# The transposes of a per-pixel convolution on one Trainium2 core: in pieces of four, on a new timetable

## Chip, core and metric

The kernel runs on one core of one Trainium2 chip. The engines of the core have an instruction stream each and meet only at semaphores: TensorE (PE in the rows, with its weight loads as PEld), VectorE (DVE), ScalarE (ACT), GpSimd (POOL) and the DMA queue of SyncE (SP). The metric is the device time of one execution in microseconds, the median over runs.

## What is computed

Eight images of 128 channels and 128 x 128 pixels pass through two layers. The first (a windowed attention and a pointwise network) isn't touched. The second, cut to its core:

```python
enh  = conv_depthwise_3x3(conv1x1(x))                   # 128 channels
h    = conv_grouped_3x3(x); h1, h2 = split(h)           # 8 and 8 channels
att  = conv1x1(h1 * h2) * attgamma + conv1x1'(x)        # 16 coefficients a pixel
# a kernel of its own at each pixel: 64 groups of 2 channels, 9 taps
attk = einsum('bpn,nm->bpm', att, selfw)                # p = pixel
y    = einsum('bpgij,bpgj->bpgi', attk, patches(enh)) + einsum('bpn,nc->bpc', att, selfb)
out  = y * ga1 + enh + x
```

The sum over taps and over the two channels of a group is what the change touches.

## The kernel before

The convolution stage works in 64 bands of 16 rows, eight to an image. A band has 4 chunks (index `j`) of 4 rows, 512 pixels, one PSUM bank. With 9 taps that makes 36 kernels, numbered `q = 9 * j + tap`. For each `q`:

- TensorE makes the pixel kernels in two matmuls of 512 columns (`basis_kernels`, L1022), into one of only two double banks `ps_k`, one half for each of the two channels of a group;
- VectorE multiplies them with the shifted `enh` (`product`, L1247), 128 x 1024 values. For 10 of the 36 (`VECTOR_MERGES`) the product stays in `ps_k` and a second VectorE instruction adds it to the next product (`merge`, L1253). The others are stored in one of 13 places of `products`. Six pairs (`POOL_MERGES`) are added up by GpSimd (L946);
- the 20 stored results that are left, the **terms**, are added up by TensorE: it transposes each row of a term into the PSUM bank `ps_t` of the chunk, accumulating (`add_term`, L1039). A term has two halves of four rows. The half `s = 0` is turned by `ident`, the half `s = 1` by `ident_swap`, which swaps the two channels. After the last term of a chunk come four transposes of `x` itself (`x_own`, L1047). This is the residual. ScalarE copies the finished bank to `summedT` (L1137), TensorE turns it back and adds the bias (`back`, L1054 and L1056), ScalarE copies it to `out_sb` (L1142), and SyncE stores it.

VectorE's 46 instructions of a band (36 products, 10 merges) are the clock of the stage. Their places 0 to 45 are the **slots**. The kernel `q` may be made as soon as its double bank is free, so it stands in the slot of the instruction that frees it (`KERNEL_SLOT`). K0 to K35 are the 36 pairs of matmuls below.

All engines work on several bands at once, in a software pipeline of four parts: band `l` is loaded, `m` gets its coefficients and `enh`, `n` is convolved, `o` is finished. In what order an engine issues its work is fixed by tables of slots:

- TensorE goes through the slots 0 to 45 and issues in each: the kernels of the slot, the terms whose `TERM_SLOT` it is (both halves, eight transposes in a row), the `back` of `BACK_SLOTS`, two matmul groups of the grouped convolution for each entry of `CONV_SLOTS` (L1004; the profile shows four records for an entry, since each of these matmuls makes two passes), the coefficients (L1011) in slot 28, and a pointwise chunk (L981) in each of `PW_SLOTS`. A number of 46 or more means the next step.
- ScalarE sorts its work by place. `TAP_PLACES` has the 18 tap products of the depthwise convolution (L1157 and L1162), and the copies of sums and outputs follow one slot after their matmuls.
- GpSimd adds 16 taps a band (L940), at places 0 to 15, and its six merges stand between them by `POOL_MERGE_PLACES`.
- Everything waits by counting semaphores. The wait stands in front of the instruction, and each engine runs in order, so that whatever stands behind it waits too.

## Time and profile before

| | us |
|---|---|
| median of 3 runs | 5569.37 (5568.04 to 5569.73) |
| profiled execution: device time | 5569.1 |
| its span, first to last instruction | 5567.0 |
| TensorE busy | 5405.1 (97%) |
| VectorE busy | 5175.4 (93%) |
| GpSimd busy | 4224.4 (76%) |
| ScalarE busy | 3301.8 (59%) |

The first 1900 us are the first layer. The convolution stage fills the rest, 64 bands one after the other. The mean granted clock of TensorE over the span is 0.996 of full speed. A VectorE instruction's duration in the rows is longer than the distance to the next start, so distances from start to start tell more than durations and idle times do.

### The profile page before, as it was taken

The numbers are of one execution on the slowest core, as the hardware profiler recorded it, in microseconds if no ns is written. First come the engines' busy times: TensorE is split into PE (matmuls) and PEld (weight loads), VectorE is DVE, ScalarE is ACT, GpSimd is POOL, SyncE is SP. The second block draws the span as 40 slices with busy tenths as digits, with TensorE's granted clock in tenths as the row PEclk, the third lists the DMA queues.
The fourth block names the chain that finished last, engine by engine and source line by source line (L and its number), as shares of the span: only waits on it lengthen the run. The fifth ranks groups of instructions, "written<-read, shape, count | busy, mean of one in ns | idle before, by whom it ended". The sixth has DMA issues, their size and how long they took to land.

```text
span 5567.0 us, 112695 instructions
## 1 busy us (share of the span) xinstructions
PE 5405.1 (97%) x37904; PEld 3895.4 (70%) x37904; DVE 5175.4 (93%) x5424; ACT 3301.8 (59%) x4094; POOL 4224.4 (76%) x1958
## 2 busy tenths in 40 slices
...
GB/s 94 71 75 75 75 75 75 70 74 75 75 75 64 78 74 79 73 78 70 81 68 75 75 73 79 73 79 68 80 70 72 81 73 78 69 82 67 72 80 46
DMA packets 175615, 413.21 MB, mean 74 GB/s; under 512 B 37200, under 2 KB 58768, under 8 KB 175504
## 3 DMA queue, kind: packets, MB, share of 16 engines
...
q14 instruction: 18, 0.15, 0.0%
...
## 4 chain that ended last, share of the span: by engine, by line
PE 45%; DVE 17%; issue 4%; DVEq 0%; DMA 0%; ACT 0%
PE ps_k L1022 19%; PE ps_t L1039 12%; DVE products L1247 10%; PE ps_m L1004 8%; DVE products L1253 4%; PE ps_p L981 3%; PE ps_t L1047 2%; PE ps_t L1056 1%; DVE ps_k L1247 1%; PE ps_t L1054 1%; DVE h_prod L1267 1%; DVEq L120 0%; DVE products L1216 0%; DMA edge_rows<-products 0%; DVE basis L329 0%
## 5 line engine op out<-in xcount | busy, mean ns | idle before, releaser
L940 POOL TENSOR_TENSOR enh<-enh,tap 128x1024 f32<-128x1024 f32 x1024 | 2258.6, 2206 | 431.3 <-ACT tap L1162 393.1
L1247 DVE TENSOR_TENSOR products<-ps_k,enh 128x1024 f32<-128x1024 f32 x1664 | 2002.9, 1219 | 71.9 <-PE ps_k L1022 36.9
L1022 PE MATMUL ps_k<-att,basis 128*128 128x512 f32 x4608 | 1710.8, 457 | 105.3 <-DVE products L1247 42.6
L1022 PEld LDWEIGHTS ps_k<-att,basis 128*128 128x128 f32 x4608 | 713.1, 189 | 873.9 <-DVE products L1247 553.4
L473 POOL TENSOR_TENSOR hidden_lo<-hidden,hidden_hi 128x1024 fp32r<-128x1024 f32 x256 | 692.8, 2726 | 717.7 <-DVE hidden_hi L678 717.7
L1162 ACT ACTIVATE tap<-e,dw 128x1024 f32<-128x1024 f32 x1024 | 1137.0, 1142 | 7.9 <-POOL enh L940 7.9
L946 POOL TENSOR_TENSOR products<-products 128x1024 f32<-128x1024 f32 x384 | 915.2, 2383 | 118.6 <-DVE products L1247 118.6
L1247 DVE TENSOR_TENSOR ps_k<-ps_k,enh 128x1024 f32<-128x1024 f32 x640 | 784.6, 1226 | 28.6 <-PE ps_k L1022 28.4
L1253 DVE TENSOR_TENSOR products<-ps_k,products 128x1024 f32<-128x1024 f32 x640 | 783.7, 1225 | 21.9
L1039 PE MATMUL ps_t<-ident_swap,products 128*128 128x128 f32 x5120 | 768.1, 273 | 0.0
L1039 PE MATMUL ps_t<-ident,products 128*128 128x128 f32 x5120 | 766.6, 272 | 0.0
L1039 PEld LDWEIGHTS ps_t<-ident,products 128*128 128x128 f32 x5120 | 628.2, 141 | 130.9 <-issue 0.2
L1039 PEld LDWEIGHTS ps_t<-ident_swap,products 128*128 128x128 f32 x5120 | 599.5, 141 | 0.0
L1137 ACT ACTIVATE summedT<-ps_t 128x512 f32<-128x512 f32 x256 | 153.1, 598 | 750.1 <-PE ps_t L1047 749.8
L1004 PE MATMUL ps_m<-xin,gT 128*32 128x512 f32 x4608 | 593.3, 607 | 0.0
L643 ACT ACTIVATE hidden<-ring,bias 128x512 f32<-128x512 f32 x512 | 350.2, 690 | 176.2 <-PE ring L501 175.3
L695 DVE CAST x_hi<-xt 128x512 fp32r<-128x512 f32 x256 | 408.2, 1635 | 47.2 <-PE ring L501 47.2
L1142 ACT ACTIVATE out_sb<-ps_t 128x512 f32<-128x512 f32 x256 | 153.2, 599 | 483.4 <-PE ps_t L1056 483.4
L498 PE MATMUL ring<-x_hi,w_hi 128*128 128x512 f32 x1024 | 418.9, 409 | 6.3 <-ACT hidden L643 3.7
L478 POOL TENSOR_TENSOR x_lo<-xt,x_hi 128x512 fp32r<-128x512 f32 x256 | 378.0, 1497 | 55.9 <-DVE x_hi L695 55.9
L501 PE MATMUL ring<-x_lo,w_hi 128*128 128x512 f32 x1024 | 404.5, 395 | 0.4 <-POOL x_lo L478 0.4
L499 PE MATMUL ring<-x_hi,w_lo 128*128 128x512 f32 x1024 | 403.1, 394 | 0.0
...
## 6 DMA issues: line engine op xcount, KB each, us to landing
...
xt<-in_x SPq DMA_DIRECT2D x128, 512.0 KB, 4.1
layer_out<-xo SPq DMA_DIRECT2D x128, 512.0 KB, 2.9
x_own<-layer_out SPq DMA_DIRECT2D x128, 512.0 KB, 3.9
...
att<-att_hi SPq DMA_DIRECT2D x512, 32.0 KB, 1.9
att<-att_lo SPq DMA_DIRECT2D x512, 32.0 KB, 2.0
...
```

Source lines behind the costliest of these rows:

```text
L473: nc.gpsimd.tensor_tensor(hidden_lo[:, h, :, :], hidden[:, h, :, :], hidden_hi[:, h, :, :].bitcast(FP32), ALU.subtract).then_inc(hidden_lo ...
L498: nc.tensor.matmul(out, w_hi[:, w, :], hi, start=start, stop=False)
L501: return nc.tensor.matmul(out, w_hi[:, w, :], lo, start=False, stop=stop)
L695: nc.vector.tensor_copy(windows(x_hi[:, PAIRS * h:PAIRS * (h + 1), :]), half_windows(xt[p], h)).then_inc(x_hi_ready, 1)
L940: nc.gpsimd.tensor_tensor(own, own, tap_sb[add % TAP_BUFFERS][:, 0:hi - lo, :], ALU.add).then_inc(dw_done, 1)
L946: nc.gpsimd.tensor_tensor(lead, lead, products[:, PLACE[q + 1], :, :], ALU.add).then_inc(pool_merged, 1)
L1004: mm = nc.tensor.matmul(ps_m[32 * j:32 * j + 32, :], gT[:, t, :], xin[p][:, r:r + CHUNK_ROWS, dx:dx + W], start=(t == 0), stop=(t == TAPS ...
L1022: mm = nc.tensor.matmul(ps_k[KERNEL_BUFFER[q]][:, BANK * s:BANK * (s + 1)], basis[:, 2 * t + s, :], att[p][:, j, :], start=True, stop=True)
L1039: mm = nc.tensor.matmul(ps_t[j % 2][:, C * r:C * (r + 1)], products[:, PLACE[q], s, C * r:C * (r + 1)], turn[:, :], is_transpose=True, sta ...
L1162: nc.scalar.activation(tap_sb[add % TAP_BUFFERS][:, 0:hi - lo, :], src, ACT.Copy, scale=dw[:, t:t + 1]).then_inc(tap_ready, 1)
L1247: nc.vector.tensor_tensor(out, kernels, enh[p][:, r:r + CHUNK_ROWS, dx:dx + W].unsqueeze(1).to_broadcast([C, 2, CHUNK_ROWS, W]), ALU.mult) ...
L1253: nc.vector.tensor_tensor(both, ps_k[KERNEL_BUFFER[q]][:, :], both, ALU.add).then_inc(product_ready, 1)
```

## The change

`add_term` becomes `add_half`: each half of a term, four transposes, is a piece with a slot of its own (`HALF_SLOT`, two entries for a term), and the residual is a piece with a slot too (`X_SLOTS`). Each piece has a wait of its own. The first piece of a chunk starts the accumulation and the last one, the residual in all four chunks, stops it and raises `sum_done`. The places of the six GpSimd merges, of the tap products, of some entries of `CONV_SLOTS`, of the pointwise chunk 2 (26 to 27), of `ATT_LOW` (32 to 33), of the first `back` (23 to 21) and of `clear_outside` (62 to 64) are new. `PLACE` gets a rule for lengths that don't divide, and `SWAPPED` one for a band that ends with its two double banks exchanged. With these tables `PLACE` is what it was, and `SWAPPED` is 0. What is computed, and how many instructions of each kind there are, stays the same.

```diff
-TERM_SLOT = {0: 7, 3: 6, 4: 11, 7: 11, 8: 12, 10: 19, 12: 16, 13: 25, 16: 23, 17: 22, 19: 27, 20: 31, 23: 32, 24: 38, 26: 35, 28: 39, 29: 44, 32: 43, 34: 47, 35: 47}
+HALF_SLOT = {0: 10, 1: 7, 6: 6, 7: 6, 8: 11, 9: 9, 14: 11, 15: 11, 16: 12, 17: 12, 20: 15, 21: 19, 24: 15, 25: 18, 26: 25, 27: 25, 32: 22, 33: 22, 34: 22, 35: 22, 38: 26, 39: 28, 40: 31, 41: 31, 46: 33, 47: 32, 48: 37, 49: 37, 52: 35, 53: 35, 56: 38, 57: 38, 58: 44, 59: 44, 64: 44, 65: 43, 68: 47, 69: 48, 70: 47, 71: 47}
+X_SLOTS = [16, 25, 38, 48]
+HALVES_OF = [sorted([(HALF_SLOT[2 * q + s], q, s) for q in TERMS if q // TAPS == j for s in range(2)] + [(X_SLOTS[j], Q, 0)]) for j in range(CHUNKS)]
-BACK_SLOTS = [23, 34, 40, 51]
+BACK_SLOTS = [21, 34, 40, 51]
-POOL_MERGE_PLACES = (0, 1.6, 4.5, 8.0, 10.5, 12.9)
+POOL_MERGE_PLACES = (0, 0.6000000000000001, 3.0, 6.0, 9.5, 10.9)
-TAP_PLACES = ((2.0, 2.0, 6.0, 7.0, 10.0, 14.0, 14.5, 15.5, 20.0), (24.0, 24.5, 26.0, 26.5, 31.0, 36.5, 37.0, 38.5, 40.5))
-CLEAR_PLACE = 62
+TAP_PLACES = ((0.5, 1.5, 3.0, 5.5, 10.5, 13.0, 13.5, 14.0, 19.5), (22.0, 24.5, 27.0, 28.0, 31.0, 35.5, 36.5, 36.5, 41.5))
+CLEAR_PLACE = 64
-ATT_LOW = 32
-CONV_SLOTS = [34, 34, 41, 41, 41, 41, 46, 46, 50, 50, 54, 54, 59, 59, 60, 60, 66, 66]
+ATT_LOW = 33
+CONV_SLOTS = [33, 33, 42, 42, 42, 42, 46, 46, 50, 50, 54, 54, 59, 59, 59, 59, 66, 66]
-PW_SLOTS = [17, 19, 26, 30, 36]
+PW_SLOTS = [17, 19, 27, 30, 36]
...
+                def add_half(n, j, half):
+                    slot, q, s = half
+                    start, stop = half == HALVES_OF[j][0], half == HALVES_OF[j][-1]
+                    if q == Q:
+                        pe.wait_ge(own_in[j // 2], 16 * n + 16)
...
+                    if start:
                         at_least(pe, out_ready, CHUNKS * n + j - 1)
...
+                    for r in range(CHUNK_ROWS):
+                        rows = x_own[j // 2][:, CHUNK_ROWS * (j % 2) + r, :] if q == Q else products[:, PLACE[q], s, C * r:C * (r + 1)]
+                        mm = nc.tensor.matmul(ps_t[j % 2][:, C * r:C * (r + 1)], rows, (ident, ident_swap)[s][:, :], is_transpose=True,
+                                              start=(start and r == 0), stop=(stop and r == CHUNK_ROWS - 1), skip_group_check=True)
+                        if r == CHUNK_ROWS - 1 and q != Q and half == LAST_HALF[q]:
+                            mm.then_inc(pool_term_done if q in POOL_MERGES else term_done, 1)
+                    if stop:
                         mm.then_inc(sum_done, 1)
```

In `HALF_SLOT` the key is `2 * q + s`. T4.1 below is the half `s = 1` of term 4, X0 the residual of chunk 0. In the rows of the changed kernel L1035 is what L1022 was, L1055 what L1039 and L1047 were, L1017 what L1004 was, and on GpSimd L953 and L959 stand for L940 and L946.

**First place, TensorE, slots 12 to 16.** Before, in order: K11, both halves of term 8, X0, K12, eight matmuls of the grouped convolution, K13 and K14, and term 12.

```order
L1022 MATMUL ps_k<-att,basis 128x512 x2
L1039 MATMUL ps_t<-ident,products 128x128 x4
L1039 MATMUL ps_t<-ident_swap,products 128x128 x4
L1047 MATMUL ps_t<-ident,x_own 128x128 x4
L1022 MATMUL ps_k<-att,basis 128x512 x2
L1004 MATMUL ps_m<-xin,gT 32x512 x8
L1022 MATMUL ps_k<-att,basis 128x512 x4
L1039 MATMUL ps_t<-ident,products 128x128 x4
L1039 MATMUL ps_t<-ident_swap,products 128x128 x4
```

Now X0 is gone from between term 8 and K12. Behind K13 stand a half of term 10 and one of term 12, and X0 follows K14. Two halves, T4.1 and T0.0, have moved to the front of this stretch, into the slots 9 and 10.

```order
L1035 MATMUL ps_k<-att,basis 128x512 x2
L1055 MATMUL ps_t<-ident,products 128x128 x4
L1055 MATMUL ps_t<-ident_swap,products 128x128 x4
L1035 MATMUL ps_k<-att,basis 128x512 x2
L1017 MATMUL ps_m<-xin,gT 32x512 x8
L1035 MATMUL ps_k<-att,basis 128x512 x2
L1055 MATMUL ps_t<-ident,products 128x128 x8
L1035 MATMUL ps_k<-att,basis 128x512 x2
L1055 MATMUL ps_t<-ident,x_own 128x128 x4
```

**Second place, TensorE, slots 41 to 45, the end of a band.** Before: K34, eight matmuls of the grouped convolution, K35, term 32, K0 of the next band, term 29, K1.

```order
L1022 MATMUL ps_k<-att,basis 128x512 x2
L1004 MATMUL ps_m<-xin,gT 32x512 x8
L1022 MATMUL ps_k<-att,basis 128x512 x2
L1039 MATMUL ps_t<-ident,products 128x128 x4
L1039 MATMUL ps_t<-ident_swap,products 128x128 x4
L1022 MATMUL ps_k<-att,basis 128x512 x2
L1039 MATMUL ps_t<-ident,products 128x128 x4
L1039 MATMUL ps_t<-ident_swap,products 128x128 x4
L1022 MATMUL ps_k<-att,basis 128x512 x2
```

Now one half of term 32 stands behind K0 instead of in front of it. (Further on, in slot 1, behind K3, three pieces stand where five stood: T34.1 and X3 follow one slot later, with no kernel in between.)

```order
L1035 MATMUL ps_k<-att,basis 128x512 x2
L1017 MATMUL ps_m<-xin,gT 32x512 x8
L1035 MATMUL ps_k<-att,basis 128x512 x2
L1055 MATMUL ps_t<-ident_swap,products 128x128 x4
L1035 MATMUL ps_k<-att,basis 128x512 x2
L1055 MATMUL ps_t<-ident,products 128x128 x4
L1055 MATMUL ps_t<-ident_swap,products 128x128 x4
L1055 MATMUL ps_t<-ident,products 128x128 x4
L1035 MATMUL ps_k<-att,basis 128x512 x2
```

**Third place, GpSimd, from the first tap of a step on.** `enh<-enh,tap` is a tap's addition, `products<-products` a merge. Before: one tap, merge 0, one tap, merge 4, three taps, merge 13, four taps.

```order
L940 TENSOR_TENSOR enh0<-enh0,tap0 128x8x128
L946 TENSOR_TENSOR products<-products 128x1024
L940 TENSOR_TENSOR enh0<-enh0,tap1 128x8x128
L946 TENSOR_TENSOR products<-products 128x1024
L940 TENSOR_TENSOR enh0<-enh0,tap2 128x8x128
L940 TENSOR_TENSOR enh0<-enh0,tap3 128x8x128
L940 TENSOR_TENSOR enh0<-enh0,tap0 128x8x128
L946 TENSOR_TENSOR products<-products 128x1024
L940 TENSOR_TENSOR enh0<-enh0,tap1 128x8x128
L940 TENSOR_TENSOR enh0<-enh0,tap2 128x8x128
L940 TENSOR_TENSOR enh0<-enh0,tap3 128x8x128
```

Now the merges 0 and 4 stand side by side behind the first tap, and merge 13 stands in front of the fifth tap, no longer behind it. So one tap more is left for the time behind merge 13.

```order
L953 TENSOR_TENSOR enh0<-enh0,tap0 128x8x128
L959 TENSOR_TENSOR products<-products 128x1024 x2
L953 TENSOR_TENSOR enh0<-enh0,tap1 128x8x128
L953 TENSOR_TENSOR enh0<-enh0,tap2 128x8x128
L953 TENSOR_TENSOR enh0<-enh0,tap3 128x8x128
L959 TENSOR_TENSOR products<-products 128x1024
L953 TENSOR_TENSOR enh0<-enh0,tap0 128x8x128
L953 TENSOR_TENSOR enh0<-enh0,tap1 128x8x128
L953 TENSOR_TENSOR enh0<-enh0,tap2 128x8x128
L959 TENSOR_TENSOR products<-products 128x1024
```

## Rows read from the trace of the kernel before

**Rows 1.** The page: busy time of an engine, share of the span, instructions.
```profile
PE 5405.1 (97%) x37904; PEld 3895.4 (70%) x37904; DVE 5175.4 (93%) x5424; ACT 3301.8 (59%) x4094; POOL 4224.4 (76%) x1958
```

**Rows 2.** One line's instructions: duration ns min/median/max, first to last start.
```profile
L1267 DVE SCALAR_TENSOR_TENSOR h_prod<-ps_m,bias_h,h_up x64: 741/742/751, 1878.2 to 5483.2; 128x512 f32<-128x512 f32 x64
```

**Rows 3.** Busy time of PE, PEld, DVE, ACT, POOL in 56 us.
```profile
2106.00:2162.00 56.00, 54.62 (x343) 35.98 (x343) 54.23 (x48) 28.45 (x34) 47.87 (x22) 1.00 0.25 76
```

**Rows 4.** VectorE's timeline: start, duration, line, operation, [idle before, releaser].
```profile
4010.24 1.22 DVE L1247 TENSOR_TENSOR ps_k<-ps_k,enh 128x1024 f32<-128x1024 f32 x1
...
4017.57 3.91 DVE L1247 TENSOR_TENSOR products<-ps_k,enh 128x1024 f32<-128x1024 f32 x3
...
4025.36 2.36 DVE L1247 TENSOR_TENSOR products<-ps_k,enh 128x1024 f32<-128x1024 f32 x2 [0.26 <-PE ps_k L1022]
...
4028.77 1.22 DVE L1247 TENSOR_TENSOR products<-ps_k,enh 128x1024 f32<-128x1024 f32 x1
4030.02 1.22 DVE L1253 TENSOR_TENSOR products<-ps_k,products 128x1024 f32<-128x1024 f32 x1
4031.16 1.22 DVE L1247 TENSOR_TENSOR products<-ps_k,enh 128x1024 f32<-128x1024 f32 x1
4032.62 1.23 DVE L1247 TENSOR_TENSOR ps_k<-ps_k,enh 128x1024 f32<-128x1024 f32 x1 [0.25 <-PE ps_k L1022]
4033.76 1.22 DVE L1247 TENSOR_TENSOR products<-ps_k,enh 128x1024 f32<-128x1024 f32 x1
...
4037.67 1.22 DVE L1247 TENSOR_TENSOR products<-ps_k,enh 128x1024 f32<-128x1024 f32 x1 [0.29 <-PE ps_k L1022]
```

**Rows 5.** TensorE's timeline: the end of a band, and slots 7 to 13 of the next.
```profile
4014.20 0.71 PE L1022 MATMUL ps_k<-att,basis 128*128 128x512 f32 x2
...
4016.72 0.73 PE L1022 MATMUL ps_k<-att,basis 128*128 128x512 f32 x2
...
4018.07 0.71 PE L1022 MATMUL ps_k<-att,basis 128*128 128x512 f32 x2
...
4019.41 1.51 PE L1022 MATMUL ps_k<-att,basis 128*128 128x512 f32 x4
4020.85 1.07 PE L1004 MATMUL ps_m<-xin,gT 128*32 128x512 f32 x8
4021.85 0.73 PE L1022 MATMUL ps_k<-att,basis 128*128 128x512 f32 x2
...
4029.42 0.60 PE L1039 MATMUL ps_t<-ident,products 128*128 128x128 f32 x4
...
4035.60 0.60 PE L1039 MATMUL ps_t<-ident,products 128*128 128x128 f32 x4
4036.04 0.60 PE L1039 MATMUL ps_t<-ident_swap,products 128*128 128x128 f32 x4
4036.47 0.60 PE L1047 MATMUL ps_t<-ident,x_own 128*128 128x128 f32 x4
4036.83 0.71 PE L1022 MATMUL ps_k<-att,basis 128*128 128x512 f32 x2
```

**Rows 6.** TensorE's weight loads: the one that waits ahead of K11.
```profile
4035.03 0.30 PEld L1022 LDWEIGHTS ps_k<-att,basis 128*128 128x128 f32 x2 [0.36 <-DVE products L1247]
```

**Rows 7.** GpSimd's timeline of the same band: L940 a tap, L946 a merge.
```profile
4028.76 2.39 POOL L946 TENSOR_TENSOR products<-products 128x1024 f32<-128x1024 f32 x1
4031.11 4.47 POOL L940 TENSOR_TENSOR enh<-enh,tap 128x1024 f32<-128x1024 f32 x2
...
4042.55 2.38 POOL L946 TENSOR_TENSOR products<-products 128x1024 f32<-128x1024 f32 x1 [1.35 <-DVE products L1247]
```

More of the change, by code:

```diff
@@ L69 @@
     KERNEL_BUFFER[q] = KERNEL_BUFFER[FREEING[q - 2][1]]
-assert [KERNEL_BUFFER[q] for _, q in FREEING[-2:]] == [0, 1]
+SWAPPED = KERNEL_BUFFER[FREEING[-2][1]]
 KERNEL_FREE = {q: FREEING[q - 2][0] if q >= 2 else FREEING[q - 2][0] - SLOTS_IN_BAND for q in range(Q)}
@@ L81 @@
-FIRST_TERM = [min((TERM_SLOT[q], q) for q in TERMS if q // TAPS == j)[1] for j in range(CHUNKS)]
-LAST_TERM = [max((TERM_SLOT[q], q) for q in TERMS if q // TAPS == j)[1] for j in range(CHUNKS)]
-TERM_COUNT = {q: i + 1 for i, q in enumerate(sorted(VECTOR_TERMS, key=lambda q: (TERM_SLOT[q], q)))}
-BACK_SLOTS = [23, 34, 40, 51]
+HALF_SLOT = {0: 10, 1: 7, 6: 6, 7: 6, 8: 11, 9: 9, 14: 11, 15: 11, 16: 12, 17: 12, 20: 15, 21: 19, 24: 15, 25: 18, 26: 25, 27: 25, 32: 22, 33: 22, 34: 22, 35: 22, 38: 26, 39: 28, 40: 31, 41: 31, 46: 33, 47: 32, 48: 37, 49: 37, 52: 35, 53: 35, 56: 38, 57: 38, 58: 44, 59: 44, 64: 44, 65: 43, 68: 47, 69: 48, 70: 47, 71: 47}
@@ L90 @@
+X_SLOTS = [16, 25, 38, 48]
+HALVES_OF = [sorted([(HALF_SLOT[2 * q + s], q, s) for q in TERMS if q // TAPS == j for s in range(2)] + [(X_SLOTS[j], Q, 0)]) for j in range(CHUNKS)]
+LAST_HALF = {q: max((HALF_SLOT[2 * q + s], q, s) for s in range(2)) for q in TERMS}
+TERM_COUNT = {q: i + 1 for i, q in enumerate(sorted(VECTOR_TERMS, key=LAST_HALF.get))}
+POOL_TERM_COUNT = {q: i + 1 for i, q in enumerate(sorted(POOL_MERGES, key=LAST_HALF.get))}
+BACK_SLOTS = [21, 34, 40, 51]
 POOL_PLACES = 2 * (TAPS - 1)
-POOL_MERGE_PLACES = (0, 1.6, 4.5, 8.0, 10.5, 12.9)
@@ L790, in convolve @@
         att = [sb(f"att{p}", [C, CHUNKS, BANK], FP32R) for p in range(2)]
-        products = sb("products", [C, PRODUCTS, 2, BANK])
+        products = sb("products", [C, PLACES, 2, BANK])
         summedT = [sb(f"summedT{i}", [C, BANK]) for i in range(2)]
@@ L1078, in step @@
                             if band is not None:
-                                for q in sorted(TERMS, key=lambda q: (TERM_SLOT[q], q)):
-                                    if TERM_SLOT[q] == slot:
-                                        add_term(band, q)
+                                for j in range(CHUNKS):
+                                    for half in HALVES_OF[j]:
+                                        if half[0] == slot:
+                                            add_half(band, j, half)
                                 if slot in BACK_SLOTS:
```

40 lines of the change are left out of this document (13 added, 27 removed).

## The prediction, made before the changed kernel ran

> **What bounds the kernel now.** I read the shares first. TensorE is busy for 97% of the span and VectorE for 93% [rows 1], and in 56 us of the convolution stage it is 54.62 and 54.23 us, against 47.87 for GpSimd and 28.45 for ScalarE [rows 3]. So two engines run side by side, both nearly full, and neither share says which one sets the pace. The distance between bands does: an instruction that runs once a band starts 64 times between 1878.2 and 5483.2 us [rows 2], so a band takes 3605.0 / 63 = 57.22 us.
>
> Next I read VectorE's starts, since its instructions overlap at their edges (1.22 us long, next start after 1.14). A product that needn't wait is followed after 1.14 us (4032.62 to 4033.76). A merge, which needs the product just ahead of it, starts 1.25 us behind that one (4028.77 to 4030.02) [rows 4]. A band has 36 gaps of the one kind, 10 of the other, and two small instructions of 0.74 - 0.08 = 0.66 us each [rows 2]: 41.0 + 12.5 + 1.3 = 54.8 us. **VectorE therefore stands still for 2.4 us in a band**, 150 us in all. The rows with idle time name K's matmuls (L1022) as what ended it [rows 4], so TensorE delivers late. Yet TensorE also waits for VectorE: 0.36 us ahead of K11 [rows 6]. This is the shape to see: work on TensorE is not too much for the band, it stands in the wrong slots. Where a kernel sits behind a block of other work, VectorE waits, and elsewhere TensorE does.
>
> **The rule of the timetable.** K11 may start when product 10 (start 4033.76) has freed its bank. It starts at 4035.03: **1.27 us after the start of the freeing instruction** at the earliest. K12 starts at 4036.83 and product 12 at 4037.67: **a product starts 0.84 us after its kernel** at the earliest [rows 4 to 6]. Work on TensorE takes, start to start: a kernel ahead of transposes 0.57 us (4035.03 to 4035.60), a piece of four transposes 0.44 (4035.60 to 4036.04), a piece just ahead of a kernel 0.36 (4036.47 to 4036.83), eight convolution records 1.00 (4020.85 to 4021.85), a kernel and sixteen of them 2.52 (4014.20 to 4016.72) [rows 5, 6]. Two kernel slots with nothing but products lie 1.14 us apart, and the slack from bank to product is 2 x 1.14 - 1.27 - 0.84 = 0.17 us. So 0.57 + 0.36 between two kernels costs nothing, 0.57 + 0.44 + 0.36 = 1.37 makes the next kernel 0.23 late, and with a residual behind it 1.80 makes it 0.66 late. A slot of a merge gives some 1.2 us back.
>
> **What the change leaves alone.** The 20 x 8 + 16 transposes of a band, their durations, and the kernels are the same, so the sum of TensorE's work is. Added are waits: 44 pieces with one each, where 20 terms and 2 residuals had one. I price them at nothing: the start of T8.1 and that of X0, which has its own wait in front, lie 0.43 us apart, like those of T8.0 and T8.1 with no wait (0.44) [rows 5], because TensorE's queue works ahead of the array. The other side of that price is a rival below. Reused places of `products` come free later by up to three slots, but the nearest user of a place is several slots behind its last half (T10.1 in slot 19 frees the place that product 28 needs in slot 35).
>
> **Stretch by stretch.** The wait of VectorE before is the distance of two rows less the free gaps between. After it is carried forward with the rule.
>
> 1. Slots 12 to 15. Before: from product 9 (4032.62) to product 12 (4037.67) 5.05 us [rows 4], free 3 x 1.14 + 1.25 = 4.67, so a wait of 0.38. It is product 12's: K12 stands behind K11, two pieces and X0 (1.80 us). After: X0 is gone, and K12 starts 1.36 us behind K11 instead. K11 had waited 0.36 us [rows 6]. The two halves that moved into slots 9 and 10 use this: K10 starts at its earliest, and K10 with T0.0, T4.0, T7.0 and T7.1 takes 0.57 + 3 x 0.44 + 0.36 = 2.25 us, of 2.28 between the banks. **Wait 0.**
>
> 2. Slots 39 to 5, across the end of the band. Before: from product 31 (4010.24) to product 4 (4025.36) 15.12 us, free 9 x 1.14 + 3 x 1.25 = 14.0, so 1.1. After: K34 starts at its earliest, since term 24 went up one slot from between K32 and K33. With S for slot 41's start: K34 at S + 1.27, 2.52 with its sixteen records, K35 and T32.1 0.93, so K0 at S + 4.72. Its bank comes free at S + 3.53 + 1.27 = 4.80: in time. (Before, K0 followed K34 after 4018.07 - 4014.20 = 3.87 [rows 5]; now 3.53.) Then K0 with three pieces, 0.57 + 0.44 + 0.44 + 0.36 = 1.81, gives K1 at 6.61 and product 1 at 7.45, wanted at 3.53 + 3 x 1.14 = 6.95: **wait 0.5, all of it in one place.** K1 to K2 0.57, K2 and eight records 1.65: K3 at 8.83, product 3 at 9.67, wanted at 9.73. K3, four pieces and X3 take 0.57 + 4 x 0.44 + 0.36 = 2.69, so K4 at 11.52 and product 4 at 12.36, wanted at 9.73 + 1.25 + 1.14 = 12.12: **wait 0.24.** In slots 37 to 40 K31 with T24 takes 1.37 and K32 with X2 and T28 takes 1.81 up to K33: **0.2** more. In all 0.95, a gain of 0.15.
>
> 3. Slots 6 to 11. Before: from product 4 to product 9 7.26 us, free 5 x 1.14 + 1.25 = 6.95: 0.3. After: T0.0 has left slot 7, so K8 starts at its earliest and K9 behind its eight records is 0.4 late instead of 0.55. Product 9 waits 0.17 and product 6, behind K6 and B3, 0.08: 0.25, a gain of 0.05 to 0.1.
>
> 4. Slots 16 to 38. From product 12 (4037.67) to the next band's product 31 (4010.24 + 57.22 = 4067.46) 29.79 us, free 19 x 1.14 + 5 x 1.25 + 1.32 = 29.2: 0.6. After, where pieces are packed anew: K14 with X0, then K15 with P0, product 14 late by 0.3; K18 with B0, then K19 with four pieces, products 18 and 19 late by 0.2 and 0.1; 0.1 in the rest. In all 0.7, a loss of 0.1.
>
> Sum: 0.38 + 0.15 + 0.07 - 0.1 = **0.5 us a band**, from 2.4 to 1.9. My rounding at each step and the edges of the stretches leave 0.25 either way. Over 63 distances that is 32 us (16 to 47). The last band's tail gets T34.1 behind T35, 0.4 us more. The profiled execution took 5569.1 us, 0.3 below the median of the runs, so I take the sum from the median: 5569.4 - 33 = **5536 us**.
>
> **Rivals.**
>
> *GpSimd is late for T0.1 (slower).* Its merges come earlier in its own order. Merge 13 can start only when product 14 is done, and before, five taps ran ahead of it. GpSimd even then waited 1.35 us [rows 7]. Now four do, GpSimd stands longer, and the fifth tap is pushed behind it. From merge 20 (1.3 us behind product 21) to its step's end it has 3 merges of 2.35 and 9 taps of 2.24 [rows 7], 27.2 us, with 23.7 us until the next product 0: it runs 4.8 us into the next band. Then one tap and merge 0: done 9.4 us after product 0. TensorE comes to T0.1 where T0.0 stood, at 4029.42, and product 0 is the second of three from 4017.57, so started at 4018.9 [rows 4, 5]: 10.5 us. Slack 1.1 us. The point from which it decides is GpSimd 1.1 us later than I work out, since TensorE and behind it K8 stand then, at every band. K8 has some 0.25 us of its own. With 2.5 us more on GpSimd a band gets 2.5 - 1.1 - 0.25 = 1.15 us longer, 72 us: 5608. For it speaks that 4.8 us is a long overrun. Against it, that merge 13 with its wait soaks up lateness in every band.
>
> *The waits go elsewhere (no change).* Total work on TensorE is unchanged and it is busy for 54.62 of 56 us. Were it the true bound, moving pieces would bring nothing, and what stretch 1 gives the stretches 2 and 4 would take: 5569, give or take 8. Against it speaks the 0.36 us of idle time in the middle of the band [rows 6], in a stretch that ends with VectorE waiting.
>
> *The extra waits cost time (slower).* A transpose takes 0.44 / 4 = 0.11 us [rows 5]. If each of the 22 new waits showed as half of that, a band would lose 1.2 us, 76 us in all: 5612. The rows above speak against it. The Trainium skill, "Advanced Engine Details and Errata", section "Miscellaneous Facts", has 50 to 100 ns for reading a semaphore's value from a sequencer. By that, were each wait such a read and exposed, the band would lose 1.1 to 2.2 us and the kernel would end at 5605 to 5675. The distance of 0.43 us across a wait [rows 5] disagrees.
>
> **How the numbers follow.** The sum, 5520 to 5555: 0.78. Waits go elsewhere: 0.13. GpSimd late: 0.06. The waits' price: 0.03. The range for eight in ten is 5514 to 5561: it takes in the whole sum's case and a part of its neighbours. A measurement of this kernel can tell some 0.2% (11 us) from no change. Below 5558: 0.80 (with a part of the second case). Within: 0.12. Above 5580: 0.08.
>
> **What the profile will show.** If I am right: 56.7 us between bands (that once-a-band instruction's first and last start 3572 us apart); product 12 follows product 11 after 1.14 us without idle time; the largest single wait of VectorE is at product 1, about 0.5 us, and product 14 has a new one of 0.3; GpSimd stands 3 to 5 us ahead of merge 13 and never ends TensorE's wait; transposes of two halves with a wait between them start 0.11 us apart. I am wrong if GpSimd (L959) releases TensorE, if ScalarE's copy of a sum comes so late that `back` waits, or if kernels behind single pieces start more than 0.36 us behind the last piece's start.

## The result, and the profile of the changed kernel

The changed kernel takes **5519.25 us** (median of 4 runs, 5518.02 to 5522.59), the kernel before 5568.77 in the same comparison: a ratio of 0.991, 95% interval 0.990 to 0.992. The forecast was 5536 us in a range of 5514 to 5561. Direction, mechanism and range were right; the gain is 49.5 us and not 33.

The page of the changed kernel, its shares (busy us, share of the span, instructions), and one row of its costliest groups (line, engine, op, out<-in | busy, mean ns | idle before it and who ended it):

```profile
PE 5377.8 (97%) x37904; PEld 3907.0 (71%) x37904; DVE 5149.3 (93%) x5424; ACT 3324.5 (60%) x4094; POOL 4237.7 (77%) x1958
...
L1055 PE MATMUL ps_t<-ident_swap,products 128*128 128x128 f32 x5120 | 736.6, 272 | 0.7 <-POOL products L959 0.7
```

The shares tell as little as in [rows 1]: the same 97% and 93% at a kernel 50 us shorter. The instruction that runs once a band, changed kernel (duration ns min/median/max, first to last start), and the same 56 us as in [rows 3]:

```profile
L1279 DVE SCALAR_TENSOR_TENSOR h_prod<-ps_m,bias_h,h_up x64: 742/742/751, 1878.1 to 5432.1; 128x512 f32<-128x512 f32 x64
```

```profile
2106.00:2162.00 56.00, 55.00 (x351) 36.97 (x350) 54.67 (x49) 28.55 (x34) 48.89 (x23) 1.00 0.25 77
```

First and last start lie 3554.0 us apart, 56.41 us a band. In [rows 2] it was 3605.0 and 57.22. The difference of 51 us is the whole gain: nothing came from the first layer or the tail.

VectorE's timeline of one band of the changed kernel (start, duration, line, operation, [idle before, releaser]):

```profile
3593.74 1.22 DVE L1259 TENSOR_TENSOR products<-ps_k,enh 128x1024 f32<-128x1024 f32 x1
3595.38 1.23 DVE L1259 TENSOR_TENSOR products<-ps_k,enh 128x1024 f32<-128x1024 f32 x1 [0.43 <-PE ps_k L1035]
...
3600.18 2.36 DVE L1259 TENSOR_TENSOR products<-ps_k,enh 128x1024 f32<-128x1024 f32 x2
3602.61 1.23 DVE L1259 TENSOR_TENSOR ps_k<-ps_k,enh 128x1024 f32<-128x1024 f32 x1
...
3607.45 1.23 DVE L1259 TENSOR_TENSOR ps_k<-ps_k,enh 128x1024 f32<-128x1024 f32 x1
...
3610.99 1.22 DVE L1259 TENSOR_TENSOR ps_k<-ps_k,enh 128x1024 f32<-128x1024 f32 x1
3612.11 1.22 DVE L1259 TENSOR_TENSOR products<-ps_k,enh 128x1024 f32<-128x1024 f32 x1
...
3615.96 1.22 DVE L1259 TENSOR_TENSOR products<-ps_k,enh 128x1024 f32<-128x1024 f32 x1 [0.21 <-PE ps_k L1035]
...
3639.68 2.35 DVE L1259 TENSOR_TENSOR products<-ps_k,enh 128x1024 f32<-128x1024 f32 x2
3641.94 1.22 DVE L1259 TENSOR_TENSOR ps_k<-ps_k,enh 128x1024 f32<-128x1024 f32 x1
3643.07 1.22 DVE L1259 TENSOR_TENSOR products<-ps_k,enh 128x1024 f32<-128x1024 f32 x1
```

The rows are product 0, product 1 (1.64 us behind it where 1.14 is free: the largest wait), products 4 and 5, product 6, product 9, products 11 and 12 (1.12 apart, where [rows 4] has a wait), product 14 with the new wait, and products 29 to 32. TensorE's timeline of the same band, in the places that the steps speak of:

```profile
3594.53 1.20 PE L1035 MATMUL ps_k<-att,basis 128*128 128x512 f32 x4
3595.66 1.08 PE L1017 MATMUL ps_m<-xin,gT 128*32 128x512 f32 x8
3596.67 0.73 PE L1035 MATMUL ps_k<-att,basis 128*128 128x512 f32 x2
...
3599.34 1.57 PE L1035 MATMUL ps_k<-att,basis 128*128 128x512 f32 x4
...
3601.84 0.73 PE L1035 MATMUL ps_k<-att,basis 128*128 128x512 f32 x2
...
3603.98 1.04 PE L1055 MATMUL ps_t<-ident_swap,products 128*128 128x128 f32 x8
...
3606.69 0.73 PE L1035 MATMUL ps_k<-att,basis 128*128 128x512 f32 x2
...
3608.16 1.47 PE L1055 MATMUL ps_t<-ident,products 128*128 128x128 f32 x12
3609.47 0.60 PE L1055 MATMUL ps_t<-ident_swap,products 128*128 128x128 f32 x4
...
3640.95 0.72 PE L1035 MATMUL ps_k<-att,basis 128*128 128x512 f32 x2
3641.51 0.60 PE L1055 MATMUL ps_t<-ident,products 128*128 128x128 f32 x4
3641.95 0.60 PE L1055 MATMUL ps_t<-ident_swap,products 128*128 128x128 f32 x4
3642.30 0.72 PE L1035 MATMUL ps_k<-att,basis 128*128 128x512 f32 x2
```

And GpSimd's, the answer to [rows 7]: merges 0 and 4, merge 13, merge 20, and merge 29.

```profile
3601.66 4.74 POOL L959 TENSOR_TENSOR products<-products 128x1024 f32<-128x1024 f32 x2
...
3617.26 2.39 POOL L959 TENSOR_TENSOR products<-products 128x1024 f32<-128x1024 f32 x1 [4.11 <-DVE products L1259]
...
3628.02 2.39 POOL L959 TENSOR_TENSOR products<-products 128x1024 f32<-128x1024 f32 x1 [1.65 <-DVE products L1259]
...
3642.11 2.38 POOL L959 TENSOR_TENSOR products<-products 128x1024 f32<-128x1024 f32 x1 [0.45 <-DVE products L1259]
```

### The profile page after: what moved, and what is told of

Same layout as the page of the kernel before. It is cut to its first block, busy times and chain, and to the rows that moved or that the text cites. A ratio compares the mean times of both kernels' runs of the same rounds, so it can differ in the third digit from the quotient of the medians.

```text
span 5515.9 us, 112725 instructions
## 1 busy us (share of the span) xinstructions
PE 5377.8 (97%) x37904; PEld 3907.0 (71%) x37904; DVE 5149.3 (93%) x5424; ACT 3324.5 (60%) x4094; POOL 4237.7 (77%) x1958
## 4 chain that ended last, share of the span: by engine, by line
PE 48%; DVE 12%; issue 5%; POOL 1%; DVEq 0%; ACT 0%; POOLq 0%
PE ps_k L1035 18%; PE ps_t L1055 15%; PE ps_m L1017 9%; DVE products L1259 6%; PE ps_p L994 3%; DVE products L1265 3%; DVE ps_k L1259 2%; PE ps_t L1067 2%; PE ps_t L1065 1%; POOL enh L953 1%; DVE h_prod L1279 1%; DVEq L133 0%; DVEq L1252 0%; DVEq L1277 0%; PE ps_t L994 0%
## 5 line engine op out<-in xcount | busy, mean ns | idle before, releaser
L953 POOL TENSOR_TENSOR enh<-enh,tap 128x1024 f32<-128x1024 f32 x1024 | 2263.0, 2210 | 68.0 <-ACT tap L1174 9.3
L1035 PE MATMUL ps_k<-att,basis 128*128 128x512 f32 x4608 | 1682.8, 449 | 80.6 <-DVE products L1265 56.5
L959 POOL TENSOR_TENSOR products<-products 128x1024 f32<-128x1024 f32 x384 | 915.9, 2392 | 418.2 <-DVE products L1259 418.2
L1035 PEld LDWEIGHTS ps_k<-att,basis 128*128 128x128 f32 x4608 | 707.1, 189 | 689.7 <-DVE products L1259 409.7
L1055 PE MATMUL ps_t<-ident_swap,products 128*128 128x128 f32 x5120 | 736.6, 272 | 0.7 <-POOL products L959 0.7
L1055 PE MATMUL ps_t<-ident,products 128*128 128x128 f32 x5120 | 724.9, 272 | 0.1
L1055 PEld LDWEIGHTS ps_t<-ident,products 128*128 128x128 f32 x5120 | 616.6, 141 | 113.0 <-DVE products L1265 0.3
L1055 PEld LDWEIGHTS ps_t<-ident_swap,products 128*128 128x128 f32 x5120 | 603.0, 141 | 68.9 <-issue 32.8
L1017 PE MATMUL ps_m<-xin,gT 128*32 128x512 f32 x4608 | 592.0, 606 | 0.0
```

The lines of the kernel that those rows point to most:

```text
L953: nc.gpsimd.tensor_tensor(own, own, tap_sb[add % TAP_BUFFERS][:, 0:hi - lo, :], ALU.add).then_inc(dw_done, 1)
L959: nc.gpsimd.tensor_tensor(lead, lead, products[:, PLACE[q + 1], :, :], ALU.add).then_inc(pool_merged, 1)
L1017: mm = nc.tensor.matmul(ps_m[32 * j:32 * j + 32, :], gT[:, t, :], xin[p][:, r:r + CHUNK_ROWS, dx:dx + W], start=(t == 0), stop=(t == TAPS ...
L1035: mm = nc.tensor.matmul(ps_k[KERNEL_BUFFER[q] ^ (SWAPPED & p)][:, BANK * s:BANK * (s + 1)], basis[:, 2 * t + s, :], att[p][:, j, :], start ...
L1055: mm = nc.tensor.matmul(ps_t[j % 2][:, C * r:C * (r + 1)], rows, (ident, ident_swap)[s][:, :], is_transpose=True, start=(start and r == 0) ...
```

## The experiments

"Band" below is the mean distance of two product 0 over bands 5 to 60; the changed kernel has 56.39 us, the kernel before 57.18. "By starts" a wait is the mean distance from the instruction before it, over the same bands, less the free distance (1.14 us, 1.25 for a merge). The kernel before ran beside each group at 5569.4 to 5570.6 us.

### The waits of the pieces: the new code on the old timetable

```diff
-X_SLOTS = [16, 25, 38, 48]
+X_SLOTS = [12, 25, 38, 47]
-BACK_SLOTS = [21, 34, 40, 51]
+BACK_SLOTS = [23, 34, 40, 51]
...
```

`HALF_SLOT` has both halves of each term where `TERM_SLOT` had the term. All other tables are those of the kernel before; the 44 waits a band stay.

> The new code with all of the old tables: both halves of a term in the term's old slot, the residual behind the chunk's last term, 44 waits instead of 22, the same order of instructions on every engine. Theory (the gain is the timetable, a wait costs TensorE nothing): 5569 us, within 0.1% of before, VectorE's waits at the same places as before. Rival (a wait shows as half of a transpose, 0.055 us): 22 more a band cost 1.2 us, 76 us in all, 5645. Rival (the code itself, with the residual as a piece of its own, brings the gain): 5519.

Measured: 5570.84 us, ratio 1.0001 (0.9992 to 1.0011). The 22 added waits are free. The interval's end bounds each of them: 0.11% of 5570 us over 22 x 64 waits is 4 ns. One of them stands in a chain that VectorE waits for, between T8.0 and T8.1 ahead of K12, and product 12 starts 1.517 us behind product 11 with it as without it (means over the bands). The Trainium skill's 50 to 100 ns for a semaphore read ("Advanced Engine Details and Errata", "Miscellaneous Facts") isn't what such a wait costs on TensorE here.

### One piece put back: X0 in slot 12 again

```diff
-X_SLOTS = [16, 25, 38, 48]
+X_SLOTS = [12, 25, 38, 48]
```

> The new kernel with X0, the residual of chunk 0, back in slot 12 behind term 8 instead of slot 16. Theory (VectorE waits at the product whose kernel stands behind too large a block): product 12 waits 0.38 us again as it did before, and K14 no longer has a residual behind it, but product 14 still waits, since K15 and the matmuls around it then run later by as much; +0.4 us a band, 5545 us. Rival (TensorE's total work bounds the band, a block's place is indifferent): 5519 us.

Measured: 5545.32 us, ratio 0.9955 (0.9939 to 0.9972). One number of the table gives back 26 us, 0.41 us a band. Stretch 1's term, 0.38, stands: product 12 waits 0.38 us again, and product 14 still 0.30, as expected. So half of the change's gain hangs on the slot of this one residual, and not on the halves of the terms.

### Only the pieces, and only the other tables

In the first kernel the pieces and the tables of ScalarE and GpSimd are the new ones, `CONV_SLOTS`, `PW_SLOTS` and `ATT_LOW` the old. In the second only those three are new, and the terms are whole and where they were.

```diff
-ATT_LOW = 33
-CONV_SLOTS = [33, 33, 42, 42, 42, 42, 46, 46, 50, 50, 54, 54, 59, 59, 59, 59, 66, 66]
-PW_SLOTS = [17, 19, 27, 30, 36]
+ATT_LOW = 32
+CONV_SLOTS = [34, 34, 41, 41, 41, 41, 46, 46, 50, 50, 54, 54, 59, 59, 60, 60, 66, 66]
+PW_SLOTS = [17, 19, 26, 30, 36]
```

> The new kernel with the old slots of the grouped convolution, of pointwise chunk 2 and of att_lo (CONV_SLOTS, PW_SLOTS, ATT_LOW), so that only the transposes' pieces, the back and the ScalarE and GpSimd tables are new. Theory (neither table alone gives the gain, because a block moved next to another block is late again): the old convolution group in slot 34 and chunk 2 in slot 26 collide with pieces that moved there, VectorE waits some 0.8 us more around products 23 to 30, 57.2 us a band, 5570 us. Rival (the pieces themselves bring the gain): at most 5530 us.

> The other part alone: whole terms in their old slots, old ScalarE and GpSimd tables, and only CONV_SLOTS, PW_SLOTS and ATT_LOW new. Theory (it pays only together with the pieces): 57.1 us a band, 5565 us, with VectorE's wait at product 12 still 0.38 us. Rival (moving the convolution's matmuls brings most of the gain): at most 5540 us.

Measured: 5576.56 us, ratio 1.0012 (1.0003 to 1.0022), and 5569.25 us, ratio 1.0000 (0.9990 to 1.0009). Neither part is worth anything alone, the pieces even cost 7 us, and together they bring 50. The first kernel's new waits stand where they were expected, at products 23, 29 and 30 (0.48, 0.25 and 0.20 us by starts). A timetable is one object: its gain doesn't divide into shares of its parts.

### ScalarE's and GpSimd's tables as before

```diff
-POOL_MERGE_PLACES = (0, 0.6000000000000001, 3.0, 6.0, 9.5, 10.9)
-TAP_PLACES = ((0.5, 1.5, 3.0, 5.5, 10.5, 13.0, 13.5, 14.0, 19.5), (22.0, 24.5, 27.0, 28.0, 31.0, 35.5, 36.5, 36.5, 41.5))
-CLEAR_PLACE = 64
+POOL_MERGE_PLACES = (0, 1.6, 4.5, 8.0, 10.5, 12.9)
+TAP_PLACES = ((2.0, 2.0, 6.0, 7.0, 10.0, 14.0, 14.5, 15.5, 20.0), (24.0, 24.5, 26.0, 26.5, 31.0, 36.5, 37.0, 38.5, 40.5))
+CLEAR_PLACE = 62
```

> The new kernel with the old tables of ScalarE and GpSimd (TAP_PLACES, POOL_MERGE_PLACES, CLEAR_PLACE), so that GpSimd's merges stand where they stood and only TensorE's order is new. Theory (the gain is TensorE's order; GpSimd's merges 0 and 4 are done in time for T0.1 and T4.1 either way): 5519 us, the same as the new kernel. Rival (T0.1 and T4.1 need the earlier merges): TensorE waits for GpSimd at T4.1 in slot 9, 0.5 us or more a band, 5550 us or more.

Measured: 5523.09 us, ratio 0.9918 (0.9901 to 0.9934). A band takes 56.38 us, as in the changed kernel; the 4 us between the medians lie outside the bands 5 to 60. The gain is TensorE's order. With the old tables merge 0 is done 7.1 us after product 0, in the changed kernel after 10.3: the new GpSimd table buys no time in the band and gives away 3.2 us of slack.

### GpSimd made late: merge 0 one tap later

```diff
-POOL_MERGE_PLACES = (0, 0.6000000000000001, 3.0, 6.0, 9.5, 10.9)
+POOL_MERGE_PLACES = (1.0, 1.1, 3.0, 6.0, 9.5, 10.9)
```

> The new kernel with GpSimd's merges 0 and 4 one tap later in its order (places 1.0 and 1.1 instead of 0 and 0.6), so 2.28 us later. In the new kernel's trace merge 0 ends 0.3 us before TensorE starts T0.1. Theory (the rival of the prediction with its point of decision, GpSimd late for T0.1, is real, and lateness beyond the slack goes into the band's time but for 0.25 us): TensorE stands 2.0 us at T0.1 in each band, the band takes 1.8 us more, 5630 us. Rival (GpSimd's 4 us of idle time ahead of merge 13 take it up, or a full queue of kernels does): within 15 us of 5519.

Measured: 5634.19 us, ratio 1.0116 (1.0100 to 1.0133). One line of its list of waits (engine, line, who is waited for: us in all, times, longest), 2100 to 5400 us:

```profile
PE ps_t L1055 <- POOL products L959: 99.3, 56, 1.8
```

One tap more ahead of merge 0 turns a single wait of 0.7 us for GpSimd in the whole run into 1.8 us in nearly every band. A band takes 58.16 us, 1.77 more, where 1.8 was expected; merge 0 ends 2.25 us later, so 0.48 us were taken up. The mechanism of the GpSimd rival is real, and the changed kernel runs a fraction of a microsecond clear of it.

### Two tables worked out with the rule, both too good

If the rule of the timetable and VectorE's 54.8 us are all there is, a better table can be found with them on paper. I looked for one with whole terms and one with pieces.

```diff
-CONV_SLOTS = [33, 33, 42, 42, 42, 42, 46, 46, 50, 50, 54, 54, 59, 59, 59, 59, 66, 66]
+CONV_SLOTS = [33, 33, 41, 41, 42, 42, 45, 46, 50, 50, 54, 55, 59, 60, 60, 60, 64, 66]
...
```

> Whole terms again, no halves apart, but with a timetable laid out anew by the same rule, and with the residual as a piece that may stand apart from its chunk's last term (X_SLOTS 15, 29, 38, 49). ScalarE's and GpSimd's places as in the new kernel. Tells apart whether the halves or the freer timetable bring the gain. Theory (any block of more than 0.9 us between two kernels costs, but a slot with a merge behind it forgives one, so whole terms can be placed nearly as well): VectorE's waits add up to some 1.3 us a band, 56.0 us a band, 5495 us, faster than the changed kernel. Rival (only the halves make it possible): 5540 us or more.

```diff
-CONV_SLOTS = [33, 33, 42, 42, 42, 42, 46, 46, 50, 50, 54, 54, 59, 59, 59, 59, 66, 66]
+CONV_SLOTS = [33, 33, 41, 41, 41, 42, 46, 46, 50, 51, 54, 54, 59, 60, 60, 60, 65, 66]
...
```

> The changed kernel's code with another timetable for halves, residuals, back and convolution (X_SLOTS 22, 27, 38, 49; BACK_SLOTS 25, 35, 40, 53), worked out by the same rule: VectorE's waits left are 0.05 at product 1, 0.23 at product 3, 0.4 at product 9. Theory (VectorE's own 54.8 us are the bound and TensorE's work fits into it): 55.5 us a band, 5463 us. Rival (TensorE, busy 97 % of the span, has no more to give): not below 5505 us.

Measured: 5643.55 us, ratio 1.0132 (1.0116 to 1.0149), and 5567.30 us, ratio 0.9996 (0.9986 to 1.0006). Both misses, by 149 and 104 us. TensorE's timeline of the second shows why: first a pair of entries in one slot, then two lone entries in two slots.

```profile
3620.51 1.07 PE L1017 MATMUL ps_m<-xin,gT 128*32 128x512 f32 x8
3621.51 0.73 PE L1035 MATMUL ps_k<-att,basis 128*128 128x512 f32 x2
...
3625.48 1.05 PE L1017 MATMUL ps_m<-xin,gT 128*32 128x512 f32 x4
3626.46 0.73 PE L1035 MATMUL ps_k<-att,basis 128*128 128x512 f32 x2
3627.12 1.05 PE L1017 MATMUL ps_m<-xin,gT 128*32 128x512 f32 x4
3628.11 0.74 PE L1035 MATMUL ps_k<-att,basis 128*128 128x512 f32 x2
```

Eight records take 1.00 us, four take 0.98. An entry fills two of the four 32-column groups of the array (`ps_m[32 * j : ...]`, `128*32` in the row), a pair fills all four. The four run side by side, two do not run faster. It is not a price for turning to the convolution and back: two pairs in a row, sixteen records, take 1.87 us in the changed kernel (median), so the second eight take 0.87 and only 0.13 us is there once. So a pair taken apart costs 1 us of TensorE, and both tables took pairs apart, three and two in a band. (Where no kernel stands between two slots, as between 41 and 42 or 59 and 60, the entries still run in a row.) Put into the rule, a lone entry of 0.98 us gives, as estimates that no run shows, some 5620 to 5640 us and some 5546 us. The first comes near the run, the second is 21 us short; 12.4 us of these are a wait of VectorE on a merge of GpSimd, the rest stays open.

The Trainium skill, "TensorEngine Tiling (Array Packing)", "Overview", has up to 4x for a dimension of 32 or less. The trace agrees: one record for each of the four groups start within 0.02 us of each other and the next four 0.44 us later, as far apart as the two records of a pointwise matmul on the whole array (0.43 us). With two groups the distance stays 0.45 us, so the gain is 2 then and not 4.

### One pair taken apart

```diff
-CONV_SLOTS = [33, 33, 42, 42, 42, 42, 46, 46, 50, 50, 54, 54, 59, 59, 59, 59, 66, 66]
+CONV_SLOTS = [33, 33, 42, 42, 42, 42, 46, 46, 50, 50, 53, 54, 59, 59, 59, 59, 66, 66]
```

> The changed kernel with one number of the convolution's table changed: the eleventh entry moves from slot 54 to slot 53, so that the pair of entries in slot 54 (eight matmul records over all four 32-column groups, 1.00 us) becomes two lone entries of four records over two of the groups, one in each of two slots. Theory from the two slower tables: a lone entry takes 0.98 us, as long as the pair, so TensorE gets 1.0 us more work a band here; by the placement rules VectorE waits 0.6 us more at product 8 and 0.25 us more at merge 4 (0.9 us a band over the changed kernel): 5576 us, ratio about 1.001. Rival: four records cost half of eight (0.50 us), nothing is added and only its place moves: within 5 us of the changed kernel's 5519 us, ratio 0.991.

Measured: 5576.76 us, ratio 1.0014 (1.0004 to 1.0023), a band of 57.26. TensorE's and then VectorE's timeline of this kernel:

```profile
3631.58 1.05 PE L1017 MATMUL ps_m<-xin,gT 128*32 128x512 f32 x4
3632.56 0.73 PE L1035 MATMUL ps_k<-att,basis 128*128 128x512 f32 x2
3633.22 1.05 PE L1017 MATMUL ps_m<-xin,gT 128*32 128x512 f32 x4
3634.20 0.74 PE L1035 MATMUL ps_k<-att,basis 128*128 128x512 f32 x2
```

```profile
3633.42 1.23 DVE L1259 TENSOR_TENSOR products<-ps_k,enh 128x1024 f32<-128x1024 f32 x1 [0.56 <-PE ps_k L1035]
3634.99 1.23 DVE L1259 TENSOR_TENSOR ps_k<-ps_k,enh 128x1024 f32<-128x1024 f32 x1 [0.34 <-PE ps_k L1035]
```

Same instructions, one number of the table, and the whole gain of the change is gone (57 us). By starts, product 8 waits 0.64 us, which it had not before, and product 9 0.41 in place of 0.17. The second is the 0.25 us more that was expected, at product 9 and not at a merge.

### The search again, with pairs kept together

With pieces:

```diff
-HALF_SLOT = {0: 10, 1: 7, 6: 6, 7: 6, 8: 11, 9: 9, 14: 11, 15: 11, 16: 12, 17: 12, 20: 15, 21: 19, 24: 15, 25: 18, 26: 25, 27: 25, 32: 22, 33: 22, 34: 22, 35: 22, 38: 26, 39: 28, 40: 31, 41: 31, 46: 33, 47: 32, 48: 37, 49: 37, 52: 35, 53: 35, 56: 38, 57: 38, 58: 44, 59: 44, 64: 44, 65: 43, 68: 47, 69: 48, 70: 47, 71: 47}
-X_SLOTS = [16, 25, 38, 48]
-BACK_SLOTS = [21, 34, 40, 51]
-CONV_SLOTS = [33, 33, 42, 42, 42, 42, 46, 46, 50, 50, 54, 54, 59, 59, 59, 59, 66, 66]
+HALF_SLOT = {0: 12, 1: 7, 6: 4, 7: 4, 8: 11, 9: 9, 14: 10, 15: 12, 16: 10, 17: 11, 20: 15, 21: 23, 24: 16, 25: 20, 26: 24, 27: 21, 32: 23, 33: 25, 34: 24, 35: 23, 38: 29, 39: 28, 40: 33, 41: 35, 46: 31, 47: 33, 48: 38, 49: 38, 52: 34, 53: 35, 56: 37, 57: 38, 58: 44, 59: 44, 64: 45, 65: 43, 68: 47, 69: 47, 70: 47, 71: 47}
+X_SLOTS = [23, 25, 38, 49]
+BACK_SLOTS = [26, 32, 40, 51]
+CONV_SLOTS = [34, 34, 41, 41, 41, 41, 46, 46, 52, 52, 54, 54, 59, 59, 59, 59, 65, 65]
```

> The changed kernel with its convolution and its transposes on yet another timetable: the two matmul entries that fill all four 32-column groups for the same rows always stand in the same slot, which the two slower tables of this study did not do. Theory: VectorE's own work of 54.8 us a band is the floor, and the placement rules (kernel 1.27 us after the product that frees its place, product 0.84 us after its kernel, eight convolution records 1.00 us) say where it waits. By them this table leaves VectorE 0.5 us of waits a band: 0.05 at product 1, 0.23 at product 3, 0.20 at product 9. A band of 55.3 us, 1.1 us less than the changed kernel's 56.39 x 63 bands: 5453 us; the ratio to the kernel before about 0.979. Rival 1: TensorE, busy 97% of the changed kernel's span, has no more to give, whatever the order: nothing under 5510 us. Rival 2: GpSimd, which reaches the first merged rows only 0.3 us before TensorE takes them in the changed kernel, ends up behind, since the band gets shorter while its own work does not: the time stops at 5500 to 5520 us, with a wait of TensorE on GpSimd in the list of waits.

Measured: **5462.06 us**, ratio 0.9808 (0.9792 to 0.9825), a band of 55.47. It beats both kernels, the changed one by 57 us, and lies 9 us over the rule's 5453; both rivals are out. Its h_prod row and two lines of its waits:

```profile
L1279 DVE SCALAR_TENSOR_TENSOR h_prod<-ps_m,bias_h,h_up x64: 742/742/751, 1878.3 to 5375.3; 128x512 f32<-128x512 f32 x64
```

```profile
PEld ps_t L1055 <- POOL products L959: 55.1, 63, 1.7
...
PE ps_t L1055 <- POOL products L959: 1.1, 2, 0.8
```

TensorE was not at its bound, since the same matmuls fit into 0.9 us less a band. GpSimd is now the neighbour: it ends an idle time of the weight loads in every band, but the matmuls behind them wait 1.1 us in all. By starts VectorE waits 0.05, 0.23, 0.19, 0.05, 0.12 and 0.05 us, 0.7 in a band.

With whole terms:

```diff
+HALF_SLOT = {0: 8, 1: 8, 6: 7, 7: 7, 8: 12, 9: 12, 14: 10, 15: 10, 16: 10, 17: 10, 20: 16, 21: 16, 24: 21, 25: 21, 26: 25, 27: 25, 32: 22, 33: 22, 34: 22, 35: 22, 38: 27, 39: 27, 40: 31, 41: 31, 46: 34, 47: 34, 48: 37, 49: 37, 52: 35, 53: 35, 56: 39, 57: 39, 58: 43, 59: 43, 64: 46, 65: 46, 68: 48, 69: 48, 70: 45, 71: 45}
+X_SLOTS = [20, 29, 38, 49]
+BACK_SLOTS = [24, 32, 40, 55]
+CONV_SLOTS = [33, 33, 41, 41, 42, 42, 47, 47, 50, 50, 52, 52, 59, 59, 60, 60, 64, 64]
+PW_SLOTS = [17, 19, 26, 30, 36]
```

> The same search, but with a term's eight transposes always in one slot, as in the kernel before; pairs of convolution entries stay together. It tells whether the pieces of four are what the gain hangs on, or only a good timetable. If waits in VectorE's row are all that counts and the placement rules hold for whole terms too (a whole term is 0.88 us of TensorE ahead of a kernel instead of 0.44 us), this table leaves 0.8 us of waits a band: 0.22 at product 0, 0.10 at merge 2, 0.20 at merge 3, 0.06 and 0.19 at two products of the second third. 55.6 us a band: 5471 us, ratio 0.982. If the pieces are needed, as the change's name has it, whole terms stay near the kernel before: 5550 us or more.

Measured: 5533.51 us, ratio 0.9934 (0.9918 to 0.9951). Neither number. The 62 us over the rule's are one wait that it did not have, 1.08 us before product 16 (68 us over the bands). The timeline of all engines of this kernel, cut to that wait's chain:

```profile
3615.43 0.34 SPq L903 DMA_DIRECT2D out<-out_sb  x1
...
3616.37 0.72 SPq L863 DMA_DIRECT2D xin<-layer_out  x1
...
3623.79 1.12 PE L994 MATMUL ps_p<-xin,pwT 128*128 128x512 f32 x2 [0.70 <-DMA xin<-layer_out]
...
3625.50 1.23 DVE L1259 TENSOR_TENSOR products<-ps_k,enh 128x1024 f32<-128x1024 f32 x1 [1.08 <-PE ps_k L1035]
```

`BACK_SLOTS[3]` = 55 makes the fourth output chunk late, SyncE waits for it with the store, and the load of the next input stands behind the store. It is issued 15.7 us after product 0 and lands 7.3 us after its issue, when TensorE has been waiting for it. So one more run, with the chunk back in slot 51:

```diff
-BACK_SLOTS = [24, 32, 40, 55]
+BACK_SLOTS = [24, 32, 40, 51]
```

> The kernel with whole terms and pairs kept together, with one number changed: the fourth output chunk's way back (its four transposes, ScalarE's copy, SyncE's store) goes from slot 55 to slot 51. In that kernel VectorE waited 1.08 us a band before product 16, which the placement rules had not given: SyncE issued the output store at 3615.4 us and the load of the next input behind it in its queue at 3616.4 us, which takes 7.3 us to land, and the pointwise matmul that reads it stood at the head of TensorE's queue. In the changed kernel the same load is issued 11.5 us after product 0, and nobody waits for it. Theory: with the store four slots (4.6 us) earlier the load lands before its reader comes, and the waits that the placement rules give are all that is left: 0.22 at product 0, 0.10 at merge 2, 0.20 at merge 3, 0.14 and 0.11 at product 8 and merge 4, 0.23 at product 16, in all 1.1 us: 55.9 us a band, 5488 us, ratio 0.985. Then whole terms on a timetable as carefully made beat the changed kernel too, and the pieces of four are worth what is left to the best table with pieces, some 25 us. Rival: the load was not what it waited for, or whole terms cost something the rules do not hold: 5530 us or more, as before.

Measured: 5497.54 us, ratio 0.9870 (0.9853 to 0.9886), a band of 56.08. SyncE's queue in this kernel:

```profile
3594.53 0.34 SPq L903 DMA_DIRECT2D out<-out_sb  x1
3595.47 0.72 SPq L863 DMA_DIRECT2D xin<-layer_out  x1
```

The load is issued 11.1 us after product 0, and the wait for it is gone: product 16 waits 0.26 us where it waited 1.08. By starts VectorE waits 0.22, 0.19, 0.21, 0.18, 0.12, 0.26 and 0.13 us at the products 0, 4, 6, 8, 9, 16 and 17, 1.3 us in all where the rule gave 1.1. Whole terms on this table beat the changed kernel with its pieces by 22 us. Pieces are worth something all the same: the best table that I found with them is 35 us faster than the best without. That is a comparison of two searches, not of two bounds. And these whole terms still use one part of the change: the residual stands apart from its chunk's last term (X0 in slot 20, that term in slot 12), which the code before could not do. What whole terms would give with the residual bound to them is not tested.

## The prediction, point by point

**What bounds the kernel.** Right: VectorE's waits in the wrong slots, with TensorE nearly full beside it. They sum to 57.2 - 54.8 = 2.4 us before and 1.6 after, and the best table has 0.7.

**Stretch 1, gain 0.38.** Right. From product 9 (3607.45) to product 12 (3612.11) it is 4.66 us, the free distance, where it was 5.05; putting X0 back costs 0.41 a band.

**Stretch 2, gain 0.15.** This is the step that was mis-sized: it measured 0.50 (from product 31 to product 4, 15.13 before, 14.64 after, means over the bands). Its main wait is there, 0.49 us at product 1. The others, 0.44 us in my sum, came to 0.16:
- "0.2 in slots 37 to 40" is 0. The rule itself gives only 0.06 there (1.27 + 1.37 + 0.84 = 3.48, free 3 x 1.14 = 3.42); the rest of the 0.2 comes from no step that the prediction shows. In the run K31 starts at its earliest, 1.27 behind 3639.68. K32 follows after 1.35 (3642.30), and product 32 0.77 behind K32, not 0.84. The three make 3.39 us (3643.07), exactly three free gaps of 1.13. Behind it, K33 was at its earliest as well.
- "0.24 at product 4" is 0.16. From K1 to K3 it takes 2.14 us (3594.53 to 3596.67), not 2.22.
- The remaining 0.07 is rounding: in the state before, where I put 1.1 for 1.13, and in the result.

**"A product starts 0.84 us after its kernel."** True of product 12, from which I read it, and of the products 1 and 4 (3594.53 to 3595.38, 3599.34 to 3600.18), but not of all. Products 6 and 9 are waited for as well and start 0.77 and 0.76 us after their kernels (3601.84 to 3602.61, 3606.69 to 3607.45). In the traces it goes by where the wait for the kernel stands. Products that carry it themselves (2, 3, 6, 7, 9, 13, 18 and 33 where VectorE waits for them in one kernel or another) start 0.75 to 0.79 us after the kernel. Where a separate instruction in front of the product has that wait, because the product itself waits for its place in `products` (0, 1, 4, 8, 10, 12, 14, 19, 29, 30, 34, 35), it is 0.84 to 0.86. (Left out are kernels right behind a pointwise chunk or the coefficients, whose two matmuls stand further apart.) From the second matmul of the kernel on, it is 0.43 to 0.44 against 0.52 to 0.54 us. No run changes the waits of a product to test this.

**Stretch 3, gain 0.05 to 0.1.** It measured -0.01 (7.26 before, 7.27 after). Product 6 waits 0.14, not 0.08, product 9 0.17 as worked out.

**Stretch 4, loss 0.1.** Measured 0.08 (29.74 to 29.82), with product 14 late by 0.29 and products 18 and 19 by 0.21 and 0.10, as written.

**The sum.** 0.39 + 0.50 - 0.01 - 0.08 = 0.80 us a band, where 0.5 stood. Over 63 distances that is 50 us. It lies outside the edges that the sum gave itself (0.25 either way, 16 to 47 us); the case of the sum, 5520 to 5555, is missed by 1 us, and the range of 5514 to 5561 held because it was drawn wider than that. In this much the hit is luck. Nearly all of the error is in stretch 2. A slip besides: 63 x 0.5 is 32 us, and the tail's 0.4 us makes the gain smaller, not 33.

**The waits at nothing.** Right. Twelve transposes of several pieces start at 3608.16 and the next piece at 3609.47: 1.31 / 12 = 0.11 us, waits included; and the new code on the old table runs at 1.0001.

**GpSimd late.** It did not come to that, but by less than I wrote. Merge 0 ends near 3604.03 (half of the two merges from 3601.66), 10.3 us after product 0 and not 9.4: GpSimd's overrun was 5.7 us and not 4.8, since it also waits 0.45 us ahead of merge 29, which the sum left out, and the next product 0 comes 0.3 us sooner. T0.1 is the second four of the eight transposes at 3603.98, so at 3604.41, 10.7 us after product 0. Slack 0.4 us, where 1.1 stood. That GpSimd stands 3 to 5 us ahead of merge 13 was right (4.11), and so, nearly, was that it never ends TensorE's wait (once in the whole run, 0.7 us). The rival at 6% had deserved more: 0.7 of its 1.1 us of slack were error.

**Waits go elsewhere.** Wrong: the best table does the same work 107 us faster than the kernel before, so TensorE's total was no bound. The pieces alone and the other tables alone gave this rival's number (5576.56 and 5569.25 us) but not its reason: the new waits of the first stand behind blocks put next to each other.

**The signs.** Product 12 after 1.12 us without idle time, product 1 the largest wait, product 14 a new one: all three came. The distance of bands did not: 56.4, not 56.7 us, h_prod's ends 3554 us apart, not 3572.
